# A graph kernel's start-up: the reach of the groups worked out on GpSimd, the high parts of Wv made on VectorE

## The reference

```python
h = jnp.maximum(_layernorm(x), 0.0)
q = h @ Wq + bq;  k = h @ Wk + bk;  v = h @ Wv + bv
adj = jnp.zeros((N, N)).at[src, dst].set(1.0)
a = q @ k.T / sqrt(512);  a = a * adj + (1.0 - adj) * -1e6
x = x + softmax(a) @ v
h = jnp.maximum(_layernorm(x), 0.0)
h = agg(h @ W1 + b1)
h = relu(gamma * (h - mean) * rsqrt(var + eps) + beta)
x = x + agg(h @ W2 + b2)
```

## Time and profile before

| what | us |
|---|---|
| median of three runs | 307.56 (307.32 to 308.18) |
| the profiled execution's own time | 307.52 |
| its span, first to last instruction | 305.7 |
| TensorE busy in the span | 294.6 |
| VectorE busy | 207.3 |
| ScalarE busy | 160.0 |
| GpSimd busy | 58.3 |

### The profile page before, as it was taken

The page is one execution under the profiler, slowest core; times in us unless marked ns, Lnnn a source line. Parts: engine busy times, 40 slices in busy tenths (PEclk is TensorE's granted clock), DMA queues, the critical chain, the costliest instruction groups (busy, mean ns, idle before and its releaser), DMA issues.

```text
span 305.7 us, 4839 instructions
## 1 busy us (share of the span) xinstructions
PE 294.6 (96%) x1339; PEld 227.2 (74%) x1345; DVE 207.3 (68%) x458; ACT 160.0 (52%) x266; POOL 58.3 (19%) x103
## 2 busy tenths in 40 slices
PE   7999889899998999999999999999999999999995
PEld 6777346466665888888888888887888888878884
DVE  3889999999978557865758575568344388276311
ACT  3999967989546646545444454357523044342000
POOL 5352344000000530032131420203010044100000
PEclk9999999999999999999999999999999999999999
DMA  7816040000500309444362625323102000000221
GB/s 261 306 31 179 1 140 0 1 0 2 207 0 3 69 3 233 82 96 81 93 142 47 140 51 104 64 41 69 34 20 51 0 3 0 0 2 0 110 99 69
DMA packets 42312, 21.67 MB, mean 71 GB/s; under 512 B 35760, under 2 KB 36016, under 8 KB 42288
## 3 DMA queue, kind: packets, MB, share of 16 engines
q1 hardware_dynamic: 41744, 20.33, 26.3%
q10 hardware_dynamic: 544, 1.05, 1.0%
HBM read 10.88 MB, written 2.10 MB: 42 GB/s over the span
## 4 chain that ended last, share of the span: by engine, by line
PE 83%; DVE 8%; issue 3%; ACT 2%; DVEq 2%; DMA 1%; ACTq 0%
PE ps L986 19%; PE ps L988 19%; PE ps L987 18%; PE ps L1239 10%; PE ps L1162 8%; PE ps L1052 8%; DVE src_oh L705 1%; DMA qk_raw<-L_gnn_Wk_in 1%; DVE WT L688 1%; DVE M L688 1%; DVEq L705 1%; DVE wB L673 1%; DVE dst_oh L707 1%; PE ps L1020 1%; ACT lead_oh L473 0%
## 5 line engine op out<-in xcount | busy, mean ns | idle before, releaser
L705 DVE TENSOR_SCALAR src_oh<-iota,ecol 128x512 f16 x135 | 40.1, 352 | 5.0 <-issue 3.0
L1052 PE MATMUL ps<-src_oh,dst_oh 128*128 x131 | 33.3, 382 | 4.3 <-DVE dst_oh L707 3.1
L1162 PE MATMUL ps<-cnt,qh 128*128 128x512 f32 x128 | 30.1, 391 | 0.3 <-ACT cnt L575 0.3
L1052 PEld LDWEIGHTS ps<-src_oh,dst_oh 128*128 x135 | 13.3, 103 | 22.2 <-issue 12.8
L1239 PE MATMUL ps<-qh,cnt 128*128 128x512 f32 x128 | 29.3, 390 | 0.0
L1162 PEld LDWEIGHTS ps<-cnt,qh 128*128 128x128 f32 x128 | 23.9, 188 | 5.6 <-DVE qh L865 0.7
L1239 PEld LDWEIGHTS ps<-qh,cnt 128*128 128x128 f32 x128 | 23.9, 188 | 5.3 <-DVE vb L967 0.3
L988 PE MATMUL ps<-v,pT 128*128 128x512 f32 x64 | 25.0, 390 | 0.0
L986 PE MATMUL ps<-hT,qh 128*128 128x512 f32 x64 | 24.9, 389 | 0.0
L986 PE MATMUL ps<-v,pT 128*128 128x512 f32 x64 | 24.9, 389 | 0.0
L987 PE MATMUL ps<-v,pT 128*128 128x512 f32 x64 | 24.9, 389 | 0.0
(11 more groups left out here) (186 smaller groups left out, 685.2 us busy)
## 6 DMA issues: line engine op xcount, KB each, us to landing
xt<-x_in SPq DMA_DIRECT2D x16, 256.0 KB, 3.3
out<-xt SPq DMA_DIRECT2D x8, 256.0 KB, 2.1
qk_raw<-L_gnn_Wk_in ACTq DMA_DIRECT2D x2, 512.0 KB, 4.9
qk_raw<-L_gnn_Wq_in SPq DMA_DIRECT2D x2, 512.0 KB, 6.7
wB_raw<-L_gnn_Wv_in SPq DMA_DIRECT2D x2, 512.0 KB, 9.0
wB_raw<-L_gnn_W_in SPq DMA_DIRECT2D x2, 512.0 KB, 4.1
w_raw<-L_gnn_W_in SPq DMA_DIRECT2D x2, 512.0 KB, 4.3
bias_row<-L_gnn_b_in SPq DMA_DIRECT2D x2, 256.0 KB, 4.6
```

The lines of the kernel that those rows point to most:

```text
L705: dve.tensor_scalar(src_oh[:, bass.ds(slot, 1), j, :].rearrange("p a n -> p (a n)"), iota[:, :], ecol[:, bass.ds(c + j, 1)], None, ALU.is_ ...
L1052: m = pe.matmul(ps[:, i % 2, :], dst_oh[:, bass.ds(slot, 1), :, j].rearrange("p a n -> p (a n)"), lead_oh[:, i % 2, j, :] if first and ACT ...
L1162: m = pe.matmul(bank(g), qh[:, d, a, c * P:(c + 1) * P], cnt[:, d, n * HALF:(n + 1) * HALF], start=(d == 0 and a == 1), stop=last)
```

## The change

ScalarE copies bank 1 (both extremes, 128x256) to a new SBUF tile `span` as the first thing it does. GpSimd does the comparing and multiplying in a new `reach_of_groups`, ahead of its first `targets_of`; VectorE's `limits` waits for that and begins with the maximum. ScalarE's copies of Wv go; VectorE makes each high part itself, directly ahead of the low part.

```diff
+         ("hit", [P, 2, NCH], F32), ("reach", [P, 2, NCH], F32), ("span", [P, 2, NCH], F32)])
@@ gpsimd, ahead of pool.wait_ge(S["ecol_ready"], 2)
+        def reach_of_groups():
+            pool.wait_ge(S["tables_ready"], 1)
+            pool.wait_ge(S["span_ready"], 1)
+            step(pool.tensor_scalar(hit[:, 0, :], span[:, 0, :], win0[:, 1:2], 0.0, ALU.is_le, ALU.add))
+            step(pool.tensor_scalar(hit[:, 1, :], span[:, 1, :], win0[:, 0:1], 0.0, ALU.is_ge, ALU.add))
+            step(pool.tensor_tensor(hit[:, 1, :], hit[:, 1, :], hit[:, 0, :], ALU.mult))
+            pool.tensor_tensor(reach[:, :, :], hit[:, 1:2, :].to_broadcast([P, 2, NCH]), chunk1[:, :, :],
+                               ALU.mult).then_inc(S["reach_ready"], 1)
+        reach_of_groups()
@@ scalar
+        act.wait_ge(S["ext_ps"], 1)
+        act.activation(span[:, :, :].rearrange("p a c -> p (a c)"), bank(1)[:, 0:2 * P], ACT.Copy).then_inc(S["span_ready"], 1)
         for item in list(start)[:8]:
             hi_of(item)
         stats(0)
         hi_of(("m", 0, 0))
-        split_w(0, (0,))
         stats(2)
         hi_of(("m", 1, 0))
-        split_w(0, (1,))
@@ vector, limits()
-            dve.wait_ge(S["tables_ready"], 1)
-            dve.wait_ge(S["ext_ps"], 1)
-            low, high = (bank(1)[:, a * P:(a + 1) * P] for a in range(2))
-            step(dve.tensor_scalar(hit[:, 0, :], low, win0[:, 1:2], None, ALU.is_le))
-            step(dve.scalar_tensor_tensor(out=hit[:, 1, :], in0=high, scalar=win0[:, 0:1], in1=hit[:, 0, :], op0=ALU.is_ge,
-                                          op1=ALU.mult))
-            step(dve.tensor_tensor(reach[:, :, :], hit[:, 1:2, :].to_broadcast([P, 2, NCH]), chunk1[:, :, :], ALU.mult))
+            dve.wait_ge(S["reach_ready"], 1)
             step(dve.tensor_reduce(lim[:, 0:2], reach[:, :, :], AX.X, ALU.max))
@@ vector
+        def wv_hi(j):
+            dve.wait_ge(S[f"wB_in{j}"], 16)
+            dve.tensor_copy(weight_load(0, j, "hi"), weight_load(0, j, "raw")).then_inc(S["w_hi"], 1)
...
-        split_w(0, 0)
-        split_w(0, 1)
+        for j in range(LOADS):
+            wv_hi(j)
+            split_w(0, j)
```

More of the change, by code:

```diff
@@ L95, in gnn_kernel @@
     hold("region_WT", 32)
-    v, zT, edge_i, edge_f, chunk1, hit, reach = shared(
+    v, zT, edge_i, edge_f, chunk1, hit, reach, span = shared(
         [("v", [P, NT, 2, D], F32R)], [("zT", [P, 2, KC, N], F32R)],
         [("edge_i", [P, 2, P], I32), ("edge_f", [P, 2, P], F32), ("chunk1", [P, 2, NCH], F32),
-         ("hit", [P, 2, NCH], F32), ("reach", [P, 2, NCH], F32)])
+         ("hit", [P, 2, NCH], F32), ("reach", [P, 2, NCH], F32), ("span", [P, 2, NCH], F32)])
     hold("region_v", 32)
@@ L161, in gnn_kernel @@
     ident_zeroed ident_ready zeros_ready pad_ready iota_ready tables_ready consts
-    dst_in src_in ext_ready ext_ps edge_f_ready ecol_ps ecol_ready drel_ready lim_ready lim_ps bounds_ready
+    dst_in src_in ext_ready ext_ps reach_ready span_ready edge_f_ready ecol_ps ecol_ready drel_ready lim_ready lim_ps bounds_ready
     x_in0 x_in1 x_in2 x_in3 qk_bias_in bcol_in bias_in b1_in
```

## The result

The changed kernel takes 309.29 us (309.11 to 310.81, eight runs) where the one before takes 307.99 (307.32 to 308.64, eight runs). The ratio is 1.0051 with a 95% interval of 1.0033 to 1.0069, that is 1.0 to 2.1 us slower. The profiled executions are 309.32 and 307.52 us, with spans of 307.5 and 305.7.

The account below looks back on a forecast made before the run. VectorE was taken to bound the kernel from 20.1 to 42 us. 307.52 + 1.46 for copies + 0.2 for one-hots + 0.1 for contention made 309.3, less a possible 0.1 later: 309.2 us, range 308.3 to 310.5.

Parts of the forecast that it names:

- What bounds the kernel: From 20.1 to 42 us VectorE bounds the chain; each microsecond more there is one more for the end.
- The 0.1 us that group 3 was to give back: GpSimd's eight targets from 43.7 to 48.5 us meet 1.7 us less of group 3, which may give back 0.1.
- Part 1: Three instructions leave VectorE's limits at 10.52 us; 1.22 us become a wait for TensorE's transpose, gain 0.
- Part 2: The reach on ScalarE and GpSimd, some 2.3 us on GpSimd from about 5.2 to 7.5 us, is covered: cost 0.
- Part 3: ScalarE loses two copies of 1.05 us; its idle time before h 0 at 24.42 us grows, gain 0.
- one-hots 0.2: GpSimd's five targets start about 0.9 us earlier, beside group 1's last one-hots on VectorE, which lose 0.2 us.
- Part 4: VectorE gains two copies of Wv behind line 770 at 20.13 us, 0.73 us each with gap, 1.46 us.
- Rival C: The copies of Wv run at one element per cycle, 2 x 1.25 + 0.3 = 2.8 us, so 310.3; chance 0.1.
- The contention rule: GpSimd's targets share something with VectorE and slow each copy of Wv by 0.06 us, 0.1 in all.
- The sum: 307.52 + 1.46 (copies) + 0.2 (one-hots beside targets) + 0.1 (copies beside targets) = 309.3 us.
- Rival D: Ring of one-hots or 0.3 us waits after 43 us absorb part; under 0.9 us arrives, 308.2; chance 0.07.
- the distance at 43 us is not the distance at the end: Sign of being wrong: the two kernels' timelines should differ by a constant once the chain returns to TensorE at 44.7 us.

Follow-up runs that it names:

- e1: Kernel before with only the reach moved to GpSimd, ScalarE keeping the copies of Wv: median 308.05 us against 307.72, ratio 1.002.
- e8: Changed kernel with item 8's low part moved ahead of VectorE's wait for the transposed limits: median 309.37 us, ratio 1.0042.
- e5: Changed kernel with GpSimd's five targets waiting until both low parts of Wv are made: ratio 1.0033 to the kernel before.
- e6: Kernel before with two register loads moved from behind to ahead of VectorE's eight low parts: median 307.52 us against 308.41, ratio 0.9976.
- e10: Kernel before with three memsets of an unused column at VectorE's start: median 309.10 us against 308.59, ratio 1.0021.
- e9: Changed kernel with two memsets of an unused column at VectorE's start: median 309.78 us against 308.59 of the kernel before, ratio 1.0032.
- e3: Changed kernel with each cast of Wv done twice in a row on VectorE: 312.09 us, ratio 1.0148.

## Why the prediction was right, and where its steps were off

The forecast was 309.2 us in 308.3 to 310.5, and slower with 0.85. Measured: 309.29, and slower by 1.0 to 2.1 us. The sum was built on the profiled execution: 1.7 us on 307.52, where 1.80 were measured. Its own steps:

- **What bounds the kernel**: right for the place, not for the price. The cost came in on VectorE between 19 and 27 us, and the distance at the end of group 2 (1.32 us in v 2) is that at 203 us (1.33 in D). But "each microsecond more on VectorE is one more for the end" did not hold: 1.70 us at h 0 became 1.32. The 0.1 us that group 3 was to give back did not come either.
- **Part 1, the limits, 0**: right, and shown alone by e1. The 1.22 us are the 1.29 us of wait ahead of `lohi`. e8 shows that filling them would not help either, since a path of 2.2 us from `lohi` through the register loads to the first one-hots holds what follows; the prediction had counted only TensorE's order.
- **Part 2, the reach, 0**: right. The copy took 0.38 us in ScalarE's idle time. GpSimd's comparisons took 0.78 and 0.73 us instead of the 0.43 that were read from a multiplication of 132 elements; the chain ended at 8.3 instead of 7.5, with cover left: the first three targets started at 8.31, as before.
- **Part 3, ScalarE relieved, 0, and one-hots 0.2**: right. ScalarE idles 1.01 us before h 0. Its layer norm did not move up as far as was said, since half of it waits for VectorE's product at 20.39; nothing hung on that. The one-hots lost 0.24 by the distance from `lohi` to the layer-norm product (6.97 against 6.73), and e5 gave back 0.45 us for one-hots and casts together, where the terms were 0.3.
- **Part 4, two casts, 1.46 us**: right. 0.68 and 0.78 with their gaps make 1.53, in which 0.1 is contention. Rival C falls: no cast ran at 1.2 us.
- **The contention rule**: GpSimd can be held for a whole instruction of VectorE (2455 ns then, up to 1989 for a target now), VectorE was only slowed. By the rule of the Trainium skill (SBUF — State Buffer, "Who interferes with whom") the second party waits for the whole instruction of the first. The changed kernel's first cast was the second by the records and did not wait, and the measurement decides.
- **The sum, +1.76 at h 0**: 1.70 measured. The step that failed is the claim that no slack stands behind it. In the kernel before, VectorE came to the ring's first reused slot 0.36 us after it was free, because of a pause of 0.75 us for register loads ahead of the one-hots; in the changed kernel the pause is gone and those 0.36 us were used up. Rival D, which had 0.07, named that ring; it was right in kind, with 0.4 us instead of 0.9. The argument against it, that VectorE never waited for the ring before 42.51, was true and did not exclude it: not to wait for a slot means to come later than the slot, and by how much was not asked.
- **The last stretch**: not in the prediction at all. 0.45 us came from where VectorE's instructions lie. The two omissions, -0.4 and +0.45, cancelled, and the predicted time is closer to the measured one than its terms are. The line "the distance at 43 us is not the distance at the end" was given as a sign of being wrong, and it came true for the last hundred microseconds. That the time fits to 0.1 us is luck, then; that it lies in the range is not.

## What to carry to other kernels

Moving work off an engine is worth what lies behind it in its own order: here the next wait was for a transpose that another engine's order held, so 1.2 us freed ahead of it bought nothing, while of the 1.70 us lost behind it 1.33 were paid. When an engine never waits for a ring, ask by how much it comes late, because that is slack for everyone upstream; and look for register loads that stand behind the last wait of a block, since moving them ahead gained what the slack had hidden (e6). For effects under a microsecond compare distances inside the profiled executions, and check a stretch that the edit does not touch: a constant that appears there is not the edit's own doing.

## What was not expected of the hardware

- **A pause that depends on where instructions lie.** VectorE pauses 0.36 us longer ahead of one of the aggregation's instructions in seven of the first ten kernels profiled and not in the other three. The instruction stands behind a branch of the program (line 932 before). Three memsets at the start bring it into the kernel before (e10), two take it out of the changed one (e9). That the fetching of instructions is the mechanism is only argued; the rows show the place and the time.
- **TensorE's clock after short idle times.** After idle times of 1.71 and 1.19 us with 1.25 us of transposes between them the granted clock was 0.50 for about 3 us (e3), at a cost of 1.40 us. After 0.28 and 1.18 us it was 1.00 in the changed kernel and 0.50 in e8, whose waits were the same. What ran between the last matmul of group 1 and the first "v" were transposes alone: for 1.9 us in the kernel before (23.9 to 25.84), 3.6 in the changed one, 5.0 in e3. The change thus brought the kernel nearer to this loss, and an idle time that costs nothing in one execution cost 1.60 us of matmul time in another.
- **From the instruction that stores the limits to the first one that uses them: 2.2 us** on VectorE, the same whether or not other work stands between (13.42 to 15.63, 13.30 to 15.51).
- **GpSimd's comparison with a per-partition operand** (one value for each of the 128 partitions) took 0.73 and 0.78 us for 128 elements, a multiplication by a constant of 132 elements 0.43.
